# A fused two-layer convolution block on one core: another order of the work inside a chunk, and of GpSimd's step in the second layer

## The chip, the cores and the metric

The kernel runs on one core of a Trainium2 chip. The metric is the device time in microseconds of one execution. Other engines are named as the profile names them: PE (TensorE), DVE (VectorE), ACT (ScalarE), POOL (GpSimd), SP (SyncE, here a DMA queue).

## The reference, cut to what matters

```python
# x: (16, 512, 64, 64) float32
# layer 0
g  = group_norm(x, groups=32)
gs = stack([sum_c(g * shifted(g, di, dj)) for di in range(5) for dj in range(5)])  # 25 maps
gs = gs / sqrt(sum(gs * gs) + 1e-6)
x  = x + relu(einsum(concat([g, gs]), W) + bias)
# layer 1
g  = group_norm(x, groups=32)
s  = relu(w2 @ relu(w1 @ mean_hw(g) + b1) + b2)          # one score a plane
q  = clip(floor(s), 0, 5)
pools = [maxpool_same(g, k) for k in (1, 3, 5, 7, 9, 11, 13)]
x  = x + (s - q) * pools[q + 1] + (q + 1 - s) * pools[q] + g
```

## The kernel before

**Layer 0** takes 16 images, each in 8 chunks (`c`) of 8 rows, so 128 chunks. Each engine runs its own list of instructions in the order in which its `image` function writes them; semaphores tie the lists together. In a chunk, PE does the picks of descriptor rows (L1253), four grams of the next chunk (`gram`, L1208, two PSUM banks in turn, so that gram 2 waits for DVE's first mask and gram 3 for its second), the norm (L1275), the descriptor part of the previous chunk's output (`tail`, L1286), 48 convolution matmuls (L1231 to L1233) and four transposes after the first 12 of them (`turn_blocks`, L1266). DVE multiplies each gram with a mask (L808), finishes the descriptor (L848, L852), takes the statistics of the finished rows (`y_stats`, L820), writes maxima over three columns (`wide_rows`, L829 to L842) and takes the statistics of a later image's x (`x_stats`, L758, four instructions a chunk). In chunk 4 it closes the next image's group statistics (`group_sums`, L768; `group_spreads`, L775 to L781), for which PE waits at L1298. ACT normalises a chunk three ahead (L595, L597), squares and takes roots (L625, L627), applies relu to the output (`conv_out`, L611) and copies the transposes (L618). POOL computes the low halves of the normalised values (`low_parts`, L447), splits the descriptor (L466, L468) and adds the residual in place (L456). Normalised chunks stand in a ring of four, so chunk c+3 may be written only when the convolution of chunk c-1 is done.

**Between the layers** the 8192 planes are sorted by class (0 to 5, the pool size) into 67 tiles of 128 planes; 5 more steps are empty.

**Layer 1** has a step for each tile t. ACT copies its planes into a padded buffer (`pad_plane`, L673 to L675), then writes the results of tile t-2 (`results`, L695, eight instructions), then the diagonals of the tile (L687). DVE pools (`pools`, L1062), PE mixes. POOL's step issues the DMAs: `gather_source(t+1)` fetches the planes of row maxima into the one buffer `source` (index copy L528, indirect DMA L531), `gather(t+2)` fetches the records and planes of y into one of four buffers (L506, index copy L507, then a branch on the class, L511, L514), `scatter(t-1)` writes a finished tile out (L539). `pad_plane(t)` waits for both fetches of its tile and for DVE to have left the padded buffer:

```python
            def pad_plane(t, u):
                act.wait_ge(gathered[u], turns_done(t, u))
                if not (isinstance(t, int) and t == 0):
                    act.wait_ge(s_rows, t)
                act.wait_ge(sourced, (t + 1) * 16)
```

`gather_source(t)` waits until the pad of tile t-1 has read `source` (s_ypad), `scatter(t)` until the eight results of its tile are written (s_res), `gather(t+2)` until the DMA of `scatter(t-2)` has landed.

## Time and profile before

| | us |
|---|---|
| median of 3 runs | 4451.67 (4446.97 to 4456.05) |
| the profiled execution, its own time | 4448.36 |
| its span | 4446.7 |
| PE busy | 3932.6 (88%) |
| DVE busy | 3557.4 (80%) |
| POOL busy | 2279.6 (51%) |
| ACT busy | 1897.6 (43%) |
| granted PE clock, mean of the span | 0.947 of full speed |
| first and last start of the picks (L1253) | 63.2, 2585.9 |
| first and last start of the pads (L673) | 2687.3, 4337.8 |

The span is read in two parts: layer 0 up to about 2610 us, layer 1 from about 2690 us. Shares of busy time are means over both.

### The profile page before, as it was taken

The numbers are of one execution on the slowest core, as the hardware profiler recorded it, in microseconds if no ns is written. First come the engines' busy times: TensorE is split into PE (matmuls) and PEld (weight loads), VectorE is DVE, ScalarE is ACT, GpSimd is POOL, SyncE is SP. The second block draws the span as 40 slices with busy tenths as digits, with TensorE's granted clock in tenths as the row PEclk, the third lists the DMA queues.
The fourth block names the chain that finished last, engine by engine and source line by source line (L and its number), as shares of the span: only waits on it lengthen the run. The fifth ranks groups of instructions, "written<-read, shape, count | busy, mean of one in ns | idle before, by whom it ended". The sixth has DMA issues, their size and how long they took to land. (4 is left out here: it accounts for less than half of the span.)

```text
span 4446.7 us, 76741 instructions
## 1 busy us (share of the span) xinstructions
PE 3932.6 (88%) x23656; PEld 2159.5 (49%) x23657; DVE 3557.4 (80%) x3528; ACT 1897.6 (43%) x2964; POOL 2279.6 (51%) x1793
## 2 busy tenths in 40 slices
PE   5999999999999999999999965789888888888785
PEld 3556555555555555655566642334333333333332
DVE  5878888788887878888888766699866799999993
ACT  3444444444454544444444403443433333433332
POOL 3555555555555655555565514355544444556442
PEclk9999999999999999999999977899998999989897
DMA  4444344544544444444453334545555566565551
GB/s 183 151 173 176 137 168 167 176 150 156 195 149 159 173 150 167 177 150 155 176 173 132 121 79 172 202 174 190 198 219 234 197 234 246 227 243 211 224 212 50
DMA packets 252235, 781.08 MB, mean 176 GB/s; under 512 B 98150, under 2 KB 98150, under 8 KB 229990
## 3 DMA queue, kind: packets, MB, share of 16 engines
q1 hardware_dynamic: 219600, 417.85, 26.9%
q0 software_dynamic: 32288, 358.95, 20.9%
q8 instruction: 176, 2.88, 0.3%
q14 instruction: 171, 1.40, 0.1%
HBM read 428.22 MB, written 409.08 MB: 188 GB/s over the span
## 5 line engine op out<-in xcount | busy, mean ns | idle before, releaser
L1062 DVE TENSOR_TENSOR arena<-arena 128x2048 f32<-128x2048 f32 (+5 forms) x539 | 1442.4, 2695 | 262.2 <-ACT arena L675 223.0
L1403 PE MATMUL psum<-arena 128*128 128x512 f32 x1072 | 608.3, 651 | 293.4 <-ACT arena L695 213.0
L1208 PE MATMUL psum<-arena 128*128 128x256 f16 (+1 forms) x6344 | 754.6, 273 | 57.4 <-DVE arena L808 44.2
L447 POOL TENSOR_TENSOR arena<-arena 128x512 f16<-128x512 f32 x512 | 720.8, 1415 | 147.1 <-ACT arena L597 141.0
L1231 PE MATMUL psum<-arena 128*128 128x512 f16 x2048 | 776.5, 379 | 0.0
L1233 PE MATMUL psum<-arena 128*128 128x512 f16 x2048 | 776.2, 379 | 0.0
L1232 PE MATMUL psum<-arena 128*128 128x512 f16 x2048 | 776.2, 379 | 0.0
L673 ACT ACTIVATE arena<-arena 128x4096 f32 x67 | 242.4, 3619 | 1051.7 <-issue 1051.7
L1208 PEld LDWEIGHTS psum<-arena 128*128 128x128 f16 x6344 | 600.3, 101 | 177.6 <-DVE arena L808 71.7
L456 POOL TENSOR_TENSOR arena<-arena 128x512 f32 (+1 forms) x512 | 635.0, 1272 | 9.0 <-ACT arena L611 6.2
L820 DVE BATCH_NORM_STATS2 bny<-arena 128x6 f32 (+1 forms) x512 | 355.6, 694 | 340.0 <-POOL arena L456 326.7
L611 ACT ACTIVATE arena<-psum,bias_sb 128x512 f32<-128x512 f32 x512 | 338.1, 686 | 581.3 <-POOL arena L456 380.1
L1407 PE MATMUL psum<-arena 128*128 128x512 f32 x1072 | 578.9, 623 | 0.0
L466 POOL CAST arena<-arena 128x128 f16<-128x128 f32 x128 | 37.3, 291 | 999.3 <-DVE arena L852 999.3
L1403 PEld LDWEIGHTS psum<-arena 128*128 128x128 f32 x1072 | 216.1, 208 | 589.7 <-issue 316.7
L1405 PE MATMUL psum<-arena 128*128 128x512 f32 x896 | 494.2, 635 | 0.0
L595 ACT ACTIVATE arena<-arena,gbias,grstd 128x512 f32 (+1 forms) x512 | 413.3, 807 | 48.6 <-POOL arena L447 45.9
L597 ACT ACTIVATE arena<-arena,gbias,grstd 128x512 f16 (+1 forms) x512 | 411.3, 803 | 0.0
L539 POOL DMA_INDIRECT out<-arena x67 | 115.4, 1722 | 544.2 <-issue 544.2
L1407 PEld LDWEIGHTS psum<-arena 128*128 128x128 f32 x1072 | 218.0, 203 | 287.7 <-issue 287.7
L808 DVE TENSOR_TENSOR arena<-psum,cst 128x256 f32<-128x256 f32 x496 | 287.1, 579 | 74.8 <-PE psum L1208 60.3
L695 ACT ACTIVATE arena<-psum,arena 128x512 f32<-128x512 f32 x536 | 319.0, 696 | 57.5 <-PE psum L1407 46.0
(161 smaller groups left out, 4324.0 us busy)
## 6 DMA issues: line engine op xcount, KB each, us to landing
arena<-in_x SPq DMA_DIRECT2D x64, 2048.0 KB, 13.2
wide_planes<-arena SPq DMA_DIRECT2D x128, 1024.0 KB, 5.4
y_planes<-arena SPq DMA_DIRECT2D x64, 2048.0 KB, 7.6
arena<-arena SPq DMA_DIRECT2D x1536, 8.0 KB, 1.8
arena<-wide_planes,arena POOLq DMA_INDIRECT x72
arena<-plane_records,arena POOLq DMA_INDIRECT x67
arena<-y_planes,arena POOLq DMA_INDIRECT x67
out<-arena POOLq DMA_INDIRECT x67, 7.9
```

Of the source, the lines that this page charges most:

```text
L447: pool.tensor_tensor(gl[:, ct, slot], g32[:, ct % 2, :], gh[:, ct, slot], ALU.subtract).then_inc(s_gl, 1)
L456: pool.tensor_tensor(y, y, relu[:, o % 2, :], ALU.add).then_inc(s_added, 1)
L595: act.activation(g32[:, ct % 2, :], piece, ACT.Identity, bias=gbias[:, ct:ct + 1], scale=grstd[:, ct:ct + 1])
L597: act.activation(gh[:, ct, (c % RING) * CW:(c % RING + 1) * CW], piece, ACT.Identity, bias=gbias[:, ct:ct + 1], scale=grstd[:, ct:ct + 1]) ...
L1062: ins = dve.tensor_tensor(dst, a, b, ALU.max)
L1208: return pe.matmul(dst, w, m, start=(k == 0), stop=(k == nk - 1))
L1231: pe.matmul(dst, h, gh[:, ct, slot], start=(ct == 0), stop=False)
L1232: pe.matmul(dst, h, gl[:, ct, slot], start=False, stop=False)
L1233: last = pe.matmul(dst, l, gh[:, ct, slot], start=False, stop=(ct == CT - 1))
L1403: pe.matmul(dst, diag[:, s, 0, :], bufs[:, u, b * CW:(b + 1) * CW], start=True, stop=False)
L1405: pe.matmul(dst, diag[:, s, 1, :], small[:, s, b * ROWS:(b + 1) * ROWS, 1:W + 1], start=False, stop=False)
L1407: pe.matmul(dst, diag[:, s, 2, :], big[:, s, b * CW:(b + 1) * CW], start=False, stop=True)\
```

## The change

Layer 0. ACT normalises the first two quarters of chunk c+3 at the start of chunk c, the third between square and root, the fourth at the end; where c+3 is the next image's first chunk, it stays late. POOL does three low parts, two residual additions, the split of the descriptor, two residual additions and the last low part. PE does the norm after the tail instead of before gram 1. DVE does the descriptor after the second mask instead of the first, the x statistics at the start of a chunk (in chunk 3 one more before the row maxima, in place of two at its end), and `group_sums` in chunk 4 behind two masks. Two copies in `wide_rows` (L831, L840) become a maximum of the same operand with itself. Layer 1. POOL's step fetches row maxima for tile t+2 instead of t+1, first; then it scatters tile t-1; then it waits for the write of tile t-2 and fetches y for tile t+2. `normalise` takes a list of quarters (`cts`) for this.

```diff
@@ -438,42 +438,49 @@
...
+            def halves(i, c):
+                n = i * CH + c
+                half = c % 2
+                pool.wait_ge(s_fn, n + 1)
+                if not (isinstance(i, int) and i == 0 and c < 2):
+                    pool.wait_ge(grouped[half], (i * (CH // 2) + c // 2) * GROUPED)
+                pool.sem_inc(s_issue, 1)
+                pool.tensor_copy(fh[:, half, :], fn).then_inc(s_th, 1)
+                pool.wait_ge(s_th, n + 1)
+                pool.tensor_tensor(fl[:, half, :], fn, fh[:, half, :], ALU.subtract).then_inc(s_t, 1)
             def image(i, first, last):
                 for c in range(CH):
-                    n = i * CH + c
-                    half = c % 2
-                    pool.wait_ge(s_fn, n + 1)
-                    if not (isinstance(i, int) and i == 0 and c < 2):
-                        pool.wait_ge(grouped[half], (i * (CH // 2) + c // 2) * GROUPED)
-                    pool.sem_inc(s_issue, 1)
-                    pool.tensor_copy(fh[:, half, :], fn).then_inc(s_th, 1)
-                    pool.wait_ge(s_th, n + 1)
-                    pool.tensor_tensor(fl[:, half, :], fn, fh[:, half, :], ALU.subtract).then_inc(s_t, 1)
-                    if c > 0:
-                        residual(i, c - 1)
-                    elif not first:
-                        residual(i - 1, CH - 1)
-                    if c + 3 < CH:
-                        low_parts(i, c + 3)
-                    elif not last:
-                        low_parts(i + 1, c + 3 - CH)
+                    ahead = (i, c + 3) if c + 3 < CH else None if last else (i + 1, c + 3 - CH)
+                    soon = ahead and c + 3 != CH
+                    back = (i, c - 1) if c else None if first else (i - 1, CH - 1)
+                    if soon:
+                        low_parts(*ahead, cts=(0, 1, 2))
+                    if back:
+                        residual(*back, outs=(0, 1))
+                    halves(i, c)
+                    if back:
+                        residual(*back, outs=(2, 3))
+                    if ahead:
+                        low_parts(*ahead, cts=(3,) if soon else range(CT))
             for c in range(3):
                 low_parts(0, c)
@@ -545,19 +552,20 @@
             def step(t, u):
-                if not (isinstance(t, int) and t + 1 >= NT):
-                    gather_source(t + 1, (u + 1) % BUFS)
+                if not (isinstance(t, int) and t + 2 >= NT):
+                    gather_source(t + 2, (u + 2) % BUFS)
+                if not (isinstance(t, int) and t < 1):
+                    scatter(t - 1, (u - 1) % BUFS)
                 if not (isinstance(t, int) and t < 2):
                     pool.wait_ge(written[(u + 2) % BUFS], ((t - 2) // BUFS + 1) * 16 if isinstance(t, int)
                                  else turn_of(t, u - 2))
                 if not (isinstance(t, int) and t + 2 >= NT):
                     gather(t + 2, (u + 2) % BUFS)
-                if not (isinstance(t, int) and t < 1):
-                    scatter(t - 1, (u - 1) % BUFS)
             gather(0, 0)
             gather_source(0, 0)
             gather(1, 1)
+            gather_source(1, 1)
             for u in range(BUFS):
                 step(u, u)
             with pool.Fori(1, NT // BUFS - 1) as g:
@@ -621,25 +628,28 @@
+                    ahead = (i, c + 3) if c + 3 < CH else None if last else (i + 1, c + 3 - CH)
+                    soon = ahead and c + 3 != CH
+                    if soon:
+                        normalise(*ahead, cts=(0, 1), first=first)
                     act.wait_ge(s_pick, n + 1)
                     act.activation(sq, psum[:, BANK_A, 0:QW], ACT.Square).then_inc(s_sq, 1)
+                    if soon:
+                        normalise(*ahead, cts=(2,))
                     act.wait_ge(s_norm, n + 1)
                     act.activation(sq, psum[:, BANK_N, 0:QW], ACT.Sqrt, bias=epsd[:, :]).then_inc(s_root, 1)
                     if not first:
                         for o in range(CT):
                             conv_out(n - 1, o)
+                    if ahead and not soon:
+                        normalise(*ahead, cts=(0, 1))
                     if c + 1 < CH:
-                        turn = lambda: after(i, c + 1)
+                        after(i, c + 1)
                     elif not last:
-                        turn = lambda: after(i + 1, 0)
-                    else:
-                        turn = lambda: None
-                    if c + 3 < CH:
-                        normalise(i, c + 3, first=first, between=turn)
-                    elif not last:
-                        normalise(i + 1, c + 3 - CH, between=turn)
-                    else:
-                        turn()
+                        after(i + 1, 0)
+                    if ahead:
+                        normalise(*ahead, cts=(3,) if soon else (2, 3))
                     if c == STATS_AT and not last:
                         group_root(i + 1)
@@ -828,7 +838,8 @@
-                dve.tensor_copy(pairs_m[:, :, :, 0:half + 1:half], y[:, :, :, 0:W:W - 1]).then_inc(s_pairs, 1)
+                dve.tensor_tensor(pairs_m[:, :, :, 0:half + 1:half], y[:, :, :, 0:W:W - 1], y[:, :, :, 0:W:W - 1],
+                                  ALU.max).then_inc(s_pairs, 1)
...
@@ -869,7 +881,15 @@
-                    between = [[lambda: descriptor(i, c)], res[0:1], res[1:2], res[2:4]]
+                    sums = [lambda: group_sums(i + 1)] if c == STATS_AT and not last else []
+                    between = [[], sums + [lambda: descriptor(i, c)], res[0:1], res[1:4]]
+                    if c == 0 and first:
+                        x_stats(1, 0)
+                        x_stats(1, 1)
+                    if c < 5 and left >= 1:
+                        x_stats(i + 1, c + 2 if c < 4 else CH - 1)
+                    elif c > 5 and left >= 2:
+                        x_stats(i + 2, c - 6)
                     if c + 1 < CH:
                         masks_of(i, c + 1, between)
                     elif not last:
@@ -880,21 +900,12 @@
                                 f()
                     if c == 0 and not first:
                         keep_stats(i - 1)
+                    if c == 3 and left >= 1:
+                        x_stats(i + 1, CH - 2)
                     if c > 0:
                         wide_rows(i, c - 1)
                     elif not first:
                         wide_rows(i - 1, CH - 1)
-                    if c == 0 and first:
-                        for e in range(3):
-                            x_stats(1, e)
-                    if c < 4 and left >= 1:
-                        x_stats(i + 1, c + 3)
-                        if c == 3:
-                            x_stats(i + 1, CH - 1)
-                    elif c > 4 and left >= 2:
-                        x_stats(i + 2, c - 5)
-                    if c == STATS_AT - 1 and not last:
-                        group_sums(i + 1)
                     if c == STATS_AT and not last:
                         group_spreads(i + 1)
                         group_values(i + 1)
@@ -1307,13 +1318,12 @@
                         pe.wait_ge(s_gl, (i * CH + min(c + 3, CH)) * CT if c + 1 < CH else ((i + 1) * CH + 2) * CT)
                         gram(nxt[0], PAIRS * nxt[1])
-                    norm(i, c, last)
-                    if nxt:
                         gram(nxt[0], PAIRS * nxt[1] + 1)
                     if c:
                         tail(i, c - 1)
                     elif not (isinstance(i, int) and i == 0):
                         tail(i - 1, CH - 1)
+                    norm(i, c, last)
                     if nxt:
                         gram(nxt[0], PAIRS * nxt[1] + 2)
                         gram(nxt[0], PAIRS * nxt[1] + 3)
```

What moves on the two engines whose order the prediction rests on. POOL in a step of layer 1's loop, before (s_ypad: a pad is done; sourced: row maxima have landed; s_res: results are written; written: a tile's write has landed):

```order
L526 ISA [waits s_ypad]
L528 ISA [waits sourced]
L528 COPY arena<-arena 128x1
L529 ISA
L531 DMA arena<-wide_planes,arena 128x4096 [waits s_src]
...
L506 MEMSET arena 128x4 [waits written3]
...
L511 DMA arena<-plane_records,arena 128x4
L514 DMA arena<-y_planes,arena 128x4096
...
L502 ISA [waits s_res]
...
L539 DMA out<-arena 8192x4096
```

and of the change:

```order
L533 ISA [waits s_ypad]
L535 ISA [waits sourced]
L535 COPY arena<-arena 128x1
L536 ISA
L538 DMA arena<-wide_planes,arena 128x4096 [waits s_src]
...
L509 ISA [waits s_res]
...
L546 DMA out<-arena 8192x4096
...
L513 MEMSET arena 128x4 [waits written3]
...
L518 DMA arena<-plane_records,arena 128x4
L521 DMA arena<-y_planes,arena 128x4096
```

The fetch of y (memory set, records, y_planes), which stood ahead of the write-out, now stands behind it. DVE in chunk 2 of the first image, from the x statistics on, before:

```order
L758 BN_STATS bnx<-arena 128x6 [waits x_loaded2]
L758 BN_STATS bnx<-arena 128x6 x3
L808 TENSOR_TENSOR arena<-psum,cst 128x2x16x8 [waits s_gram,s_pick]
L848 RECIPROCAL arena<-arena 128x128 [waits s_root]
L852 TENSOR_TENSOR arena<-psum,arena 128x128 [waits s_t,s_rinv]
L808 TENSOR_TENSOR arena<-psum,cst 128x2x16x8 [waits s_gram]
L820 BN_STATS bny<-arena 128x6 [waits s_added]
```

and of the change:

```order
L768 BN_STATS bnx<-arena 128x6 [waits x_loaded2]
L768 BN_STATS bnx<-arena 128x6 x3
L818 TENSOR_TENSOR arena<-psum,cst 128x2x16x8 [waits s_gram,s_pick]
L818 TENSOR_TENSOR arena<-psum,cst 128x2x16x8 [waits s_gram]
L860 RECIPROCAL arena<-arena 128x128 [waits s_root]
L864 TENSOR_TENSOR arena<-psum,arena 128x128 [waits s_t,s_rinv]
```

The second mask has moved ahead of the descriptor, and the x statistics stand where they stood, right ahead of the first mask.

## Rows read from the trace of the kernel before

**Rows 1.** The timeline of PE: start, us, line; chunks 0, 4, 5, 6 and the next 0
```profile
1498.18 0.82 PE L1253 MATMUL psum<-arena,cst 128*32 128x48 f32 x48
...
1576.81 0.88 PE L1253 MATMUL psum<-arena,cst 128*32 128x64 f32 x48
1602.01 0.88 PE L1253 MATMUL psum<-arena,cst 128*32 128x64 f32 x48
1620.91 0.88 PE L1253 MATMUL psum<-arena,cst 128*32 128x64 f32 x48
...
1658.01 0.82 PE L1253 MATMUL psum<-arena,cst 128*32 128x48 f32 x48
```

**Rows 2.** The timeline of PE in chunk 4 of the image before
```profile
1424.94 4.46 PE L1208 MATMUL psum<-arena 128*128 128x256 f16 x24 [2.42 <-DVE arena L808]
...
1441.88 0.38 PE L1298 MATMUL psum<-gd,cst 128*128 128x4 f32 x2 [1.55 <-DVE gd L781]
```

**Rows 3.** Table by stretch, classes 0 to 4: length, then PE, PEld, DVE, ACT, POOL
```profile
2735.00:2904.50 169.50, 131.48 (x261) 55.32 (x259) 111.20 (x50) 79.46 (x120) 64.00 (x58) 0.86 0.51 198
2904.50:3133.50 229.00, 202.32 (x436) 87.11 (x435) 213.45 (x78) 99.54 (x150) 130.81 (x70) 0.93 0.48 176
3163.50:3523.00 359.50, 300.29 (x633) 128.52 (x631) 239.95 (x80) 129.12 (x195) 174.91 (x92) 0.91 0.55 216
3523.00:3806.50 283.50, 243.07 (x529) 104.35 (x528) 258.59 (x99) 109.25 (x165) 123.24 (x77) 0.95 0.62 238
3806.50:4094.50 288.00, 248.07 (x520) 106.08 (x520) 273.12 (x88) 109.26 (x165) 172.56 (x77) 0.91 0.58 225
```

**Rows 4.** The timeline of one tile of class 3: start, us, engine, line
```profile
3579.13 4.72 ACT L695 ACTIVATE arena<-psum,arena 128x512 f32<-128x512 f32 x8
3579.46 23.99 DVE L1062 TENSOR_TENSOR arena<-arena 128x4096 f32<-128x4096 f32 x9 [1.99 <-ACT arena L675]
...
3585.51 1.74 POOL L539 DMA_INDIRECT out<-arena  x1 [7.16 <-issue]
3587.26 0.40 POOL L528 COPY arena<-arena 128x1 int32 x1
3588.56 1.24 POOL L531 DMA_INDIRECT arena<-wide_planes,arena  x1 [0.91 <-POOL arena L528]
...
3594.43 0.18 POOL L507 COPY arena<-arena 128x1 int32 x1
3596.21 3.69 POOL L511 DMA_INDIRECT arena<-plane_records,arena  x1 [1.60 <-issue]
3600.21 4.11 POOL L514 DMA_INDIRECT arena<-y_planes,arena  x1 [0.30 <-issue]
3600.72 3.62 ACT L673 ACTIVATE arena<-arena 128x4096 f32 x1 [15.76 <-issue]
...
3605.20 4.42 DVE L1062 TENSOR_TENSOR arena<-arena 128x4096 f32<-128x4096 f32 x1 [1.75 <-ACT arena L675]
```

**Rows 5.** The timeline of one tile of class 2
```profile
3482.82 4.56 POOL L531 DMA_INDIRECT arena<-wide_planes,arena  x1 [0.91 <-POOL arena L528]
...
3493.88 0.99 POOL L514 DMA_INDIRECT arena<-y_planes,arena  x1 [0.30 <-issue]
3495.76 3.62 ACT L673 ACTIVATE arena<-arena 128x4096 f32 x1 [17.61 <-issue]
```

**Rows 6.** Groups by form of DVE in the tile of class 3: xcount, busy us, mean ns
```profile
L1062 DVE TENSOR_TENSOR arena<-arena 128x4096 f32<-128x4096 f32 x3 | 13.3, 4425 | 2.1 <-ACT arena L675 2.0
L1062 DVE TENSOR_TENSOR arena<-arena 128x2048 f32<-128x2048 f32 x2 | 4.5, 2290 | 0.0
L1062 DVE TENSOR_TENSOR arena<-arena 128x1024 f32<-128x1024 f32 x3 | 3.6, 1223 | 0.1
```

**Rows 7.** The timeline of DVE: the x statistics of one chunk
```profile
1399.38 2.47 DVE L758 BATCH_NORM_STATS2 bnx<-arena 128x6 f32 x4
```

**Rows 8.** One line of DVE: its durations (ns, least, median, most)
```profile
L831 DVE COPY arena<-arena x128: 218/1168/1195, 94.1 to 2607.0; 128x64 f32 x104, 128x64 f32<-128x64 f32 x24
```

More of the change, by code:

```diff
@@ L440, in _, with low_parts @@
         def _(pool):
-            def low_parts(i, c):
+            def low_parts(i, c, cts=range(CT)):
                 n0 = (i * CH + c) * CT
                 slot = slice((c % RING) * CW, (c % RING + 1) * CW)
-                for ct in range(CT):
+                for ct in cts:
                     pool.wait_ge(s_gh, n0 + ct + 1)
@@ L448, in low_parts, with residual @@
                                        ALU.subtract).then_inc(s_gl, 1)
-            def residual(i, c):
+            def residual(i, c, outs=range(CT)):
                 n0 = (i * CH + c) * CT
-                for o in range(CT):
+                for o in outs:
                     y = xs(o, c * CW, CW, i % 2)
@@ L581, in group_root, with normalise @@
                 act.activation(grs[:, :], psum[:, BANK_N, CT:2 * CT], ACT.Sqrt, bias=epsg[:, :]).then_inc(s_gsq, 1)
-            def normalise(i, c, first=False, between=None):
+            def normalise(i, c, cts=range(CT), first=False):
                 n0 = (i * CH + c) * CT
-                act.wait_ge(s_newton, 3 * i + 3)
-                if not first:
-                    act.wait_ge(s_chunk_used, i * CH + c - RING + 1)
-                for ct in range(CT):
+                if 0 in cts:
+                    act.wait_ge(s_newton, 3 * i + 3)
+                    if not first:
+                        act.wait_ge(s_chunk_used, i * CH + c - RING + 1)
+                for ct in cts:
                     if not (isinstance(n0, int) and n0 + ct < 2):
@@ L598, in normalise @@
                                    bias=gbias[:, ct:ct + 1], scale=grstd[:, ct:ct + 1]).then_inc(s_gh, 1)
-                    if between and ct == 1:
-                        between()
             def conv_out(chunk, o):
```

3 lines of the change are left out of this document (2 added, 1 removed).

## The prediction

> **What bounds the kernel now.** The page's shares of busy time mix two layers, so I read the table by stretch first, then the timelines. In layer 0 PE bounds: its chunk starts [rows 1] show 18.9 us for a chunk that waits for nothing (1602.01 to 1620.91), and 25.2 us for chunk 4 (1576.81 to 1602.01). The reader should see how little is to be had: seven chunks of 18.9 and one shorter one (of the two from 1620.91 to 1658.01, 37.1 in all, the first takes 18.2) make a floor of 150.5 us, the image takes 159.8, so 9.3 are waits: 6.3 in chunk 4, and 3.0 in chunks 0 to 3 (78.6 less four times 18.9). In chunk 4 PE waits 2.42 for the first mask of DVE, then spends 4.46 on two grams, held up by the second mask, then waits 1.55 for the group spread [rows 2]. Some 0.4 of the 6.3 are small matmuls that stand only there, so the second mask has 6.3 - 2.42 - 1.55 - 0.4, about 1.9.
>
> In layer 1 the engines are less full: per tile 21.2, 22.9, 27.7, 25.8 and 26.2 us in classes 0 to 4 (169.5 over 8 tiles, 229 over 10, 359.5 over 13, 283.5 over 11, 288 over 11), with DVE busy 111, 213, 240, 259 and 273 of these [rows 3]. A loop through four parties sets the period where DVE is idle. It can be followed in one tile of class 3 [rows 4]: DVE starts at 3579.46; ACT writes results until 3583.85; POOL issues the write-out at 3585.51, 1.66 later (its branch on the class), then the index copy, then the fetch of row maxima, done at 3589.80; the next pad starts at 3600.72 and DVE 4.48 after it. Sum: 25.7, the period. The fetch of y in those rows (3596.21 to 3604.32) is for a tile after the one padded at 3600.72, and has a whole period to land.
>
> The same rows show what a POOL instruction costs beside DVE. The write-out ends 0.9 after a DVE instruction's end (4.43 and 2.4 after the start, that is 3586.3, and 3587.25), the index copy ends with the next one (3587.6 against 3587.66), and the fetches that begin inside the last two DVE instructions take 3.69 and 4.11, again to 0.9 past the ends of these, while one that begins when DVE is idle takes 0.99 [rows 4 to 6]. I use this throughout: a copy ends with the DVE instruction in which it begins, an indirect DMA 0.9 us after.
>
> **The change, layer 1.** The fetch of row maxima for tile t+2 now goes ahead of the write-out; it needs the pad of t+1, so it is issued as DVE starts a tile, and no longer waits for results and write-out. That takes it out of the loop. But the fetch of y for t+2 moves from before the write-out of t-1 to behind it. That write-out needs results which ACT writes only after the pad of t+1. So y, which had a period of slack, is now issued in the very period at whose end its tile is padded. The loop becomes: pad, results, write-out, fetch of y (memory set, copy, 1.6 for the branch on the class, records, 0.3, planes), landing, pad. It is longer than the old one by the records' DMA and 0.7 of branch at least. The wait for the write of t-2, which ended the idle time ahead of the old fetch, falls away at no cost.
>
> Worked for class 3, from DVE's start at 0; its instructions end at 4.4, 6.9, 8.1, 9.3, 10.6, 12.9, 15.1, 19.5, 24.0 (one of 4096, one of 2.4 us, three of 1024, two of 2048, two of 4096, in the order of the code, [rows 6]). Index copy: begins with DVE, ends 4.4. Row maxima: from 5.4 to 7.8. Write-out: ready at 6.05, behind that fetch, to 9.05. Copy to 9.3, branch, records from 11.0 to 13.8, planes from 14.1 to 16.0. From the end of the last fetch to the pad: 8.4 in class 2, where the write-out was issued 7 us before it, 10.9 in class 3, where it was just before [rows 4, 5]; the queue is shared, and here three fetches and writes stand within 8 us, so I take 9.9. With 4.5 to DVE's next start: 30.4, against 25.8. By the same steps, classes 0 and 1 (six first instructions of 2.29; write-out to 7.7, copy to 9.2, records to 12.5, planes to 14.7, landing 8.6): 27.8. Class 2 (2.3 four times, then two of 4.43): records fall into the first long one and end at 14.7, planes into the second, 19.1; with 8.6 and 4.5, 32.2. Class 4: planes end at 17.2, with 9.1 and 4.5, 30.8. Class 5 has shorter instructions in the middle: 27.4, below the 28 us that its twelve DVE instructions need (an estimate from the durations by length [rows 6] and the lengths in the code), so no change there.
>
> Sum: 6.6 x 8 = 53, 4.9 x 10 = 49, 4.5 x 13 = 59, 4.6 x 11 = 51, 4.6 x 11 = 51; first tiles, which lose too (about 19 by the same steps), less 9 that class 5's lead over DVE absorbs: 10. In all **+273 us**. PE (243 us busy over 11 tiles of class 3, 22 a tile) stays hidden, and ACT (109, 10 a tile) too [rows 3].
>
> A rule speaks against the slow fetches. In the rows, the two fetches of y under long DVE instructions take 3.69 and 4.11, and alone 0.99 [rows 4, 5]. The Trainium skill, page "SBUF — State Buffer", section "Who interferes with whom", holds that a tensor_tensor contends with GpSimd's reads but does not hold up descriptor generation (it marks the reason as inferred). By that rule the fetches would take 1 us each. The sum for layer 1 would then be the faster rival's below, -18, and not +273. This trace disagrees with it for indirect DMAs, so I go by the rows.
>
> **The change, layer 0.** No work is added or taken away; PE's floor stays. In chunk 4, two x statistics (2.5 each [rows 7]) and the group sums stood ahead of the first mask; one statistic moves ahead of the previous chunk's row maxima (same queue, so it still delays, but chunk 3 has idle time on DVE), the sums go behind two masks. The descriptor goes behind the second mask, so the wait of 1.9 for this mask goes. `low_parts` now run beside x statistics and masks instead of row maxima. What this is worth shows in the first copy of the row maxima: 1168 ns beside POOL, 218 without [rows 8]; its form as a maximum has a price between these two, and with POOL idle it is near the lower one. I expect row maxima to be about 1.7 us shorter a chunk. The norm now stands behind a gram and the tail, about 3 us later, which makes root, relu and residual later and y statistics, by my estimate, about 1 us; 0.7 a chunk is left to DVE. Chunk 4: 1.2 for the first mask, 0 for the second, 1.2 for the spread, 0.4 that always stood there: 2.8 instead of 6.3. Chunks 0 to 3: 0.8 instead of 3.0. Gain 5.7 an image, 14 such images: **-80 us**. Bounds: nothing, and all of it, 9.3 x 14.5 = 135. I take 80, since the masks' lateness is mostly queue ahead of them. Moving the norm, root and relu back costs nothing as long as relu is ready when PE has done its four grams; an estimated 2 us of cover is left there, and some 3 for the descriptor's DMAs ahead of the next tail. If these went, each of 128 chunks would pay the excess.
>
> Sum: +273 - 80 = +193. The profiled execution has 4448.4, 3.3 below the median of the runs, so 4641 profiled and **4644 us** as a median.
>
> **The rivals.**
> 1. Row maxima early wins, y costs nothing (faster): POOL's later fetches are not drawn out. Then the loop is 6.05 + 1.0 + 0.3 + 1.6 + 1.0 + 0.3 + 1.0 + 8.6 + 4.5 = 24.4 in every class, or DVE's own 25 in class 4. Against the old periods: +26, +15, -43, -15, -11, and 10: -18; with -80, 4350 + 3 = 4354. For it: the 0.99 [rows 5]. Against: DVE is in the middle of its tile when y is fetched, as in [rows 4]. It decides for faster below a mean of 1.5 us lost a tile (80 over 53).
> 2. One more DVE instruction is lost by each write-out, so that the fetch of y slips by about 2.5 us a tile: +130 more, 4775. It would be so if POOL's branch began only when the fetch of row maxima is done. In the rows the branch runs while POOL is still busy or idle, so I doubt it.
> 3. Layer 0 gains nothing, since the x statistic still precedes the masks and y statistics come later; layer 1 as forecast: 4724.
> 4. The change does not do what it says in layer 1: y lands in time because ACT's pad is bound by DVE anyway. Class 1 (213 of 229 busy) is nearest to that. Then only layer 0's gain is left, but some loss in classes 0 and 2: about 4450, no change.
>
> **How the numbers follow.** Forecast 0.70, rival 2 0.10, rival 3 0.11, rival 1 0.06, rival 4 0.03. Within the forecast, 1.5 us of error in a tile's loop is 80 us, and layer 0 may gain 50 more or less. The range 4540 to 4730 takes in the forecast's own bounds and rival 3. A measurement here can tell 0.2%, 9 us. Faster 0.06, same 0.02, slower 0.92.
>
> **What would show it.** Right: in the timeline of layer 1, POOL's fetch of y follows the write-out, and the pad starts 8 to 10 us after it ends; DVE's idle time ahead of its pooling, put down to the pad, about doubles; periods of 28, 28, 32, 30, 31 and 28. The row maxima have landed long before. In layer 0, chunk 4 takes some 21.7 us and the image about 154; the first copy's line takes well under 1 us. Wrong: pads that start without a landing just before, class periods unchanged, or fetches of y of 1 us in the middle of DVE's tile. If the sign is right and the size is not, look first at the time from the last fetch to the pad.

## The result, and the profile after

The changed kernel takes **4749.73 us** (median of 4 runs, 4744.19 to 4756.57) against 4452.97 for the kernel before on the same chip: ratio 1.0669, 95% interval 1.065 to 1.0687. The profiled spans are 4742.5 and 4446.7 us. So the sign was right, but the size is +297 us against the forecast's +193, and 4749.73 lies above the range of 4540 to 4730.

The table by stretch, classes 0 to 5 (length, then PE, PEld, DVE, ACT and POOL busy, PE clock, DMA share, GB/s):

```profile
2683.50:2912.50 229.00, 129.85 (x256) 54.79 (x256) 108.77 (x48) 79.46 (x120) 89.64 (x56) 0.78 0.37 147
2912.50:3211.50 299.00, 221.00 (x459) 94.75 (x460) 222.35 (x80) 99.31 (x150) 127.36 (x70) 0.85 0.34 135
3243.70:3663.00 419.30, 299.71 (x624) 128.32 (x624) 233.93 (x78) 127.28 (x195) 197.63 (x91) 0.85 0.50 185
3663.00:4015.50 352.50, 253.04 (x528) 108.29 (x528) 261.55 (x99) 109.24 (x165) 138.28 (x77) 0.86 0.50 191
4015.50:4376.30 360.80, 255.51 (x528) 109.29 (x528) 274.76 (x88) 109.24 (x165) 162.63 (x77) 0.84 0.48 180
4376.30:4646.20 269.90, 207.59 (x432) 89.09 (x432) 245.05 (x108) 89.41 (x136) 101.38 (x63) 0.87 0.52 196
```

The first five answer to [rows 3]: the same tiles (8, 10, 13, 11, 11, and 9 of class 5) and nearly the same busy time of DVE, in stretches longer by 60, 70, 60, 69 and 73 us. No engine has more work; all of them idle more. From the starts of the pads and the ends of POOL's fetches in the timeline, in us per tile (period: from one pad to the next):

| class | period before | forecast | after | end of y's fetch to pad, forecast | after |
|---|---|---|---|---|---|
| 0 | 21.2 | 27.8 | 28.6 | 8.6 | 8.8 |
| 1 | 22.9 | 27.8 | 29.9 | 8.6 | 8.8, in one tile 6.2 |
| 2 | 27.7 | 32.2 | 32.4 | 8.6 | 8.7 |
| 3 | 25.8 | 30.4 | 32.0 | 9.9 | 11.6 |
| 4 | 26.2 | 30.8 | 32.8 | 9.1 | 10.3 to 11.1 in seven tiles, 8.9 to 9.1 in three, 4.2 in one |
| 5 | 27.0 | no change | 30.0 | - | 10.1 |

The wait that grew, from the waits of the whole span (total, times, longest):

```profile
ACT arena L683 <- issue: 1442.5, 67, 63.8
...
DVE arena L1073 <- ACT arena L685: 612.4, 66, 16.8
```

Before, the pad (then L673) idled 1051.7 us ahead of its 67 executions, and DVE 223.0 us for the pad, 42 times. Now DVE waits for the pad in 66 of 67 tiles, and nearly three times as long, where the forecast had it double. "issue" at the pad is a DMA: the one line of the fetch of y names the pad as its waiter, 65 times, with the time from issue to landing below it:

```profile
  ACT arena L683: 1370.8, 65
...
DMA to landing us min/median/max: 6.4/11.0/12.4
```

The loop itself, in one tile of class 3, to be read beside [rows 4]:

```profile
3726.76 3.62 ACT L683 ACTIVATE arena<-arena 128x4096 f32 x1 [21.75 <-issue]
...
3731.23 23.98 DVE L1073 TENSOR_TENSOR arena<-arena 128x4096 f32<-128x4096 f32 x9 [7.73 <-ACT arena L685]
3731.43 4.27 POOL L535 COPY arena<-arena 128x1 int32 x1 [15.98 <-ACT arena L685]
...
3736.60 2.41 POOL L538 DMA_INDIRECT arena<-wide_planes,arena  x1 [0.90 <-POOL arena L535]
3739.32 1.01 POOL L546 DMA_INDIRECT out<-arena  x1 [0.30 <-issue]
3740.33 0.11 POOL L513 MEMSET arena<- 128x4 f32 x1
3740.38 0.30 POOL L514 COPY arena<-arena 128x1 int32 x1
3742.31 2.72 POOL L518 DMA_INDIRECT arena<-plane_records,arena  x1 [1.64 <-issue]
3745.34 1.82 POOL L521 DMA_INDIRECT arena<-y_planes,arena  x1 [0.31 <-issue]
3758.72 3.62 ACT L683 ACTIVATE arena<-arena 128x4096 f32 x1 [22.00 <-issue]
```

DVE starts at 3731.23. POOL issues the row maxima (L538), the write-out (L546), the records (L518) and y (L521), which ends at 3747.16, 15.9 after DVE's start, where the forecast had 16.0. DVE is done at 3755.2. The pad starts only at 3758.72, 11.6 after the fetch of y, and DVE 4.5 after the pad. The row maxima were issued 19.7 us ahead of the pad; they wait for nobody any more.

A tile of class 0, where the forecast's time for POOL was off:

```profile
2745.46 6.82 DVE L1073 TENSOR_TENSOR arena<-arena 128x2048 f32<-128x2048 f32 x3 [15.67 <-ACT arena L685]
...
2751.52 1.65 POOL L546 DMA_INDIRECT out<-arena  x1 [0.54 <-issue]
2752.44 6.82 DVE L1073 TENSOR_TENSOR arena<-arena 128x2048 f32<-128x2048 f32 x3 [0.16 <-DVE arena L1073]
2753.16 0.12 POOL L513 MEMSET arena<- 128x4 f32 x1
2753.21 1.57 POOL L514 COPY arena<-arena 128x1 int32 x1
2757.01 3.19 POOL L518 DMA_INDIRECT arena<-plane_records,arena  x1 [2.23 <-issue]
2760.50 0.98 POOL L521 DMA_INDIRECT arena<-y_planes,arena  x1 [0.31 <-issue]
2770.39 3.62 ACT L683 ACTIVATE arena<-arena 128x4096 f32 x1 [19.43 <-issue]
```

From the copy to the records' fetch, the branch on the class, POOL takes 2.23, not 1.6. The fetch begins at 2757.01, just behind the boundary between two of DVE's instructions (2752.44 and two thirds of 6.82 are 2756.99), and so lasts to 0.9 after the next one's end. The records end 14.7 us after DVE's start, where the forecast had 12.5. So it is in four of the eight tiles of class 0 (periods of 29.0 to 29.5); in the other four the branch takes 2.1 to 2.2 as well, but the fetch begins just ahead of the boundary, y ends at 14.7 as forecast, and the periods are 27.8 to 28.2.

Layer 0. PE's chunk starts in one image (chunks 0, 1, 3, 5 and the next 0):

```profile
1454.42 0.82 PE L1264 MATMUL psum<-arena,cst 128*32 128x48 f32 x48
1475.72 0.88 PE L1264 MATMUL psum<-arena,cst 128*32 128x64 f32 x48
...
1513.55 0.88 PE L1264 MATMUL psum<-arena,cst 128*32 128x64 f32 x48
1553.60 0.88 PE L1264 MATMUL psum<-arena,cst 128*32 128x64 f32 x48
...
1609.84 0.82 PE L1264 MATMUL psum<-arena,cst 128*32 128x48 f32 x48
```

Chunks 1 and 2 take 37.8 together, so 18.9 each. Chunks 3 and 4 take 40.05: chunk 4 needs 21.15 where it needed 25.2 [rows 1]. Chunk 0 needs 21.3 in this image and between 18.2 and 24.7 in the others, 20.5 in the mean, against 20.2 before. The image takes 155.4, against 159.8. From the first chunk's start to the last one's, layer 0 has 2452.8 us (62.5 to 2515.3), against 2522.1: 69 less.

Why chunk 0 gained nothing shows at an image start with a long chunk 0 (24.7 us):

```profile
1762.99 1.23 DVE L846 TENSOR_TENSOR arena<-arena 128x1024 f32<-128x1024 f32 x1 [2.13 <-DMA wide_planes<-arena]
...
1764.04 0.82 PE L1264 MATMUL psum<-arena,cst 128*32 128x48 f32 x48
...
1769.27 2.47 DVE L768 BATCH_NORM_STATS2 bnx<-arena 128x6 f32 x4 [2.08 <-issue]
1771.65 1.01 DVE L818 TENSOR_TENSOR arena<-psum,cst 128x256 f32<-128x256 f32 x2
1772.29 5.30 PE L1219 MATMUL psum<-arena 128*128 128x256 f16 x24 [2.74 <-DVE arena L818]
```

DVE waited 2.13 for a write of row maxima to land, then 2.08 with no releaser at the start of an image, and then did the x statistic of 2.47 ahead of the first mask (L818), for which PE waited 2.74. And the durations of the first copy of the row maxima, to be read beside [rows 8]:

```profile
L841 DVE TENSOR_TENSOR arena<-arena x128: 265/278/1239, 94.8 to 2539.2; 128x64 f32 x104, 128x64 f32<-128x64 f32 x24
```

### The profile page after: what moved, and what is told of

Its sections match the earlier page's. It is cut to its first block and busy times, and to the rows that moved or that the text cites. A ratio compares the mean times of both kernels' runs of the same rounds, so it can differ in the third digit from the quotient of the medians.

```text
span 4742.5 us, 76845 instructions
## 1 busy us (share of the span) xinstructions
PE 3932.9 (83%) x23656; PEld 2185.4 (46%) x23657; DVE 3364.5 (71%) x3528; ACT 1892.0 (40%) x2964; POOL 2257.0 (48%) x1793
## 5 line engine op out<-in xcount | busy, mean ns | idle before, releaser
L1413 PE MATMUL psum<-arena 128*128 128x512 f32 x1072 | 624.6, 667 | 631.3 <-ACT arena L705 590.4
L447 POOL TENSOR_TENSOR arena<-arena 128x512 f16<-128x512 f32 x512 | 651.1, 1277 | 858.0 <-ACT arena L606 856.2
L1219 PE MATMUL psum<-arena 128*128 128x256 f16 (+1 forms) x6344 | 712.3, 270 | 34.8 <-DVE arena L818 21.5
L535 POOL COPY arena<-arena 128x1 int32 (+1 forms) x72 | 192.0, 2667 | 953.7 <-ACT arena L685 939.5
L1219 PEld LDWEIGHTS psum<-arena 128*128 128x128 f16 x6344 | 588.8, 98 | 119.1 <-DVE arena L818 29.2
L1417 PE MATMUL psum<-arena 128*128 128x512 f32 x1072 | 582.0, 626 | 0.0
L1415 PE MATMUL psum<-arena 128*128 128x512 f32 x896 | 503.3, 646 | 0.0
L768 DVE BATCH_NORM_STATS2 bnx<-arena 128x6 f32 (+1 forms) x512 | 314.8, 678 | 35.7 <-issue 25.0
L818 DVE TENSOR_TENSOR arena<-psum,cst 128x256 f32<-128x256 f32 x496 | 275.7, 586 | 79.6 <-PE psum L1219 79.3
## 6 DMA issues: line engine op xcount, KB each, us to landing
arena<-wide_planes,arena POOLq DMA_INDIRECT x72, 10.6
out<-arena POOLq DMA_INDIRECT x67, 12.8
```

The costliest lines, as they stand in the source:

```text
L447: pool.tensor_tensor(gl[:, ct, slot], g32[:, ct % 2, :], gh[:, ct, slot], ALU.subtract).then_inc(s_gl, 1)
L1219: return pe.matmul(dst, w, m, start=(k == 0), stop=(k == nk - 1))
L1413: pe.matmul(dst, diag[:, s, 0, :], bufs[:, u, b * CW:(b + 1) * CW], start=True, stop=False)
L1415: pe.matmul(dst, diag[:, s, 1, :], small[:, s, b * ROWS:(b + 1) * ROWS, 1:W + 1], start=False, stop=False)
L1417: pe.matmul(dst, diag[:, s, 2, :], big[:, s, b * CW:(b + 1) * CW], start=False, stop=True)\
```

## The experiments

Twelve kernels in four groups (e1 to e4, e5 to e8, e9 to e11, e12); each group shared its runs of the kernel before. A ratio below is to those, with its 95% interval.

**e1 and e2, the two halves of the change.** e1 keeps the change's layer 0 and has the old step in layer 1; e2 the other way round.

```diff
 # e1, against the change
-                    gather_source(t + 2, (u + 2) % BUFS)
-                    scatter(t - 1, (u - 1) % BUFS)
+                    gather_source(t + 1, (u + 1) % BUFS)
                     pool.wait_ge(written[(u + 2) % BUFS], ...)
                     gather(t + 2, (u + 2) % BUFS)
+                    scatter(t - 1, (u - 1) % BUFS)
```

> The change's chunk order in layer 0, with the old GpSimd step in layer 1. The two parts lie one after the other, so their effects should add. Theory (the two spans of the trace): first to last picks 2452.8 instead of 2522.1, so 69 us faster than before, 4384 us; class periods in layer 1 as before. Rival (layer 1's loss comes in part from what layer 0 leaves behind): well off 4384.

> Layer 0 as before, with the change's GpSimd step. Theory: before plus the whole loss of layer 1, 365 us: 4818 us; periods of 28.7, 29.9, 32.4, 32.0, 32.8 and 30.0 us in classes 0 to 5. Rival as in e1: off by more than 20 us.

Measured: e1 4385.31 us, 0.9855 [0.9839, 0.9872]; e2 4825.51 us, 1.0848 [1.083, 1.0866]. The halves are -64 and +376 against their before (4449.68), together +312; the whole change has +297. So all of the loss is the step of layer 1, as expected, and the halves add up to within 15 us, a third of a per cent. Some 9 of these are in class 4: in e2 the fetch of y slips into another long instruction of DVE in six tiles (periods of 34.7 to 35.3), in the change in three.

**e3, y a whole tile earlier.** The row maxima still go first, but y is fetched for tile t+3, into the buffer of the tile that has just been written out; the wait is then for that write.

```diff
-                    pool.wait_ge(written[(u + 2) % BUFS], ((t - 2) // BUFS + 1) * 16 ...)
-                    gather(t + 2, (u + 2) % BUFS)
+                    pool.wait_ge(written[(u + 3) % BUFS], ((t - 1) // BUFS + 1) * 16 ...)
+                    gather(t + 3, (u + 3) % BUFS)
```

> The change, but the fetch of y is for tile t+3 and waits for the write of t-1: it stands behind the write-out and still has a whole period. Theory (y in the loop is the whole loss, early row maxima are a gain): periods near DVE's own work or the step's own length, about 21, 23, 22, 24.5, 25.5, 28 us; about 4300 us, below both kernels. Rival (early row maxima are worth nothing, since three transfers then land together): periods as before, 4384 us.

Measured: 4380.44 us, 0.9853 [0.9836, 0.9871]. This undoes 369 us of loss by fetching y one tile further ahead, with the row maxima still first: the theory's mechanism holds. Its number (4300) does not, and the rival's 4384 is met only in the sum, since the periods are not as before. They are 19.8, 22.3, 25.4, 27.4, 28.2 and 27.8: better than before in classes 0 to 2, worse in 3 to 5. One tile of class 3 shows why:

```profile
3604.65 0.10 POOL L513 MEMSET arena<- 128x4 f32 x1 [13.59 <-DMA out<-arena]
...
3606.58 4.85 POOL L518 DMA_INDIRECT arena<-plane_records,arena  x1 [1.61 <-issue]
...
3611.74 2.08 POOL L521 DMA_INDIRECT arena<-y_planes,arena  x1 [0.31 <-issue]
...
3615.14 1.22 POOL L538 DMA_INDIRECT arena<-wide_planes,arena  x1 [0.89 <-POOL arena L535]
```

POOL stands 13.59 us at the landing of the write, then needs 9.2 for y, of which 4.85 go into a fetch under a DVE instruction of 4.42, and only then fetches the row maxima, 13 us ahead of their pad. Here, what stands in front of the last fetch on POOL is in the loop.

**e4, y ahead of the write-out.** Row maxima, then y for t+2, then the write-out.

```diff
                     gather_source(t + 2, (u + 2) % BUFS)
-                    scatter(t - 1, (u - 1) % BUFS)
                     pool.wait_ge(written[(u + 2) % BUFS], ...)
                     gather(t + 2, (u + 2) % BUFS)
+                    scatter(t - 1, (u - 1) % BUFS)
```

> The change, with the fetch of y for t+2 ahead of the write-out of t-1, behind the fetch of row maxima. Theory (both the wait for the pad and the write-out ahead of it lengthen the loop): results and write-out leave the loop, y ends at about 12.5, 12.5, 14.7, 13.8, 15.0 us into DVE's tile, periods 25.6, 25.6, 27.8, 28.2, 28.6, 28 us: about 4520 us. Rival (only the write-out's place counts): periods as before, 4384. Rival (only the place behind the pad counts): no change, 4750.

Measured: 4590.5 us, 1.0318 [1.0301, 1.0335]. Periods 27.7, 27.3, 29.4, 29.0, 29.8 and 27.7. 159 us come back of the loss, less than expected, and neither rival's number is met. One tile of class 0:

```profile
2749.42 6.83 DVE L1073 TENSOR_TENSOR arena<-arena 128x2048 f32<-128x2048 f32 x3 [14.09 <-ACT arena L685]
...
2759.92 1.97 POOL L521 DMA_INDIRECT arena<-y_planes,arena  x1 [0.31 <-issue]
2762.19 1.93 POOL L546 DMA_INDIRECT out<-arena  x1 [0.30 <-issue]
```

The fetch of y ends 12.5 us after DVE's start, and in nearly all tiles of classes 1 to 4 at 12.5, 14.6, 13.8 and 15.0, within 0.1 of the expectation. The miss is the landing: the pad starts 10.0 to 10.8 us after that end in the mean of every class (8.7 to 8.8 in classes 0 to 2 of the change), with the write-out issued 0.3 us behind the fetch. So a transfer behind y also makes it late, and a y fetched after the pad of t+1 stayed in the loop in both places that were tried.

**e5, the long instructions of DVE cut in two**, in the changed kernel.

```diff
+                    if tuple(dst.shape)[1:] == (H, W):
+                        dve.tensor_tensor(dst[:, 0:H // 2], a[:, 0:H // 2], b[:, 0:H // 2], ALU.max)
+                        dst, a, b = (v_[:, H // 2:H] for v_ in (dst, a, b))
                     ins = dve.tensor_tensor(dst, a, b, ALU.max)
```

> The change, with each pooling instruction of 4096 elements cut into two of 2048. Theory (a GpSimd copy ends with the DVE instruction in which it begins, an indirect DMA 0.9 us after): y is fetched earlier by about 2 us in some tiles of class 1, 4.4 in class 2, 2 in classes 3 and 4: 110 us faster than the change, about 4640. Rival (pooling does not hold up the making of descriptors): the length of DVE's instructions does not matter, 4750 or a few us more for the added instructions.

Measured: 4653.58 us, 1.0457 [1.044, 1.0473], 96 us less than the change (110 expected), with the same work for DVE and none less for POOL. One tile of class 3:

```profile
3720.87 2.14 POOL L535 COPY arena<-arena 128x1 int32 x1 [16.27 <-ACT arena L685]
...
3723.90 2.16 POOL L538 DMA_INDIRECT arena<-wide_planes,arena  x1 [0.89 <-POOL arena L535]
...
3730.55 1.66 POOL L518 DMA_INDIRECT arena<-plane_records,arena  x1 [1.62 <-issue]
3732.52 1.96 POOL L521 DMA_INDIRECT arena<-y_planes,arena  x1 [0.31 <-issue]
```

The copy that lasted 4.27 beside an instruction of 4.43 lasts 2.14 beside one of 2.29, and the fetch of y ends 13.8 us after DVE's start instead of 15.9. So DVE's tensor_tensor does hold up POOL's index copies and its indirect DMAs. The Trainium skill, page "SBUF — State Buffer", section "Who interferes with whom", which keeps descriptor generation out of that, is not borne out for indirect DMAs here. Class 2 gained 2.3 us a tile and not 4.4: y is fetched earlier, as expected, but now 6.9 us behind the start of the write-out instead of 9.0, and its landing rises from 8.7 to 10.6.

**e6, the write-out taken away**, in the changed kernel.

```diff
-                    pool.indirect_dma_start(out=out_rows[:, :],
-                                            out_offset=bass.IndirectOffsetOnAxis(ap=idx[:, b:b + 1], axis=0),
-                                            in_=bufs[:, b, :], in_offset=None,
-                                            bounds_check=NPL - 1, oob_is_err=False).then_inc(written[b], 16)
+                    pool.dma_start(no_out[bass.ds(t, 1), :], bufs[0:1, b, 0:REC]).then_inc(written[b], 16)
```

> The change, but the second layer's result is not written out: the write-out of a tile is a DMA of 16 bytes. Theory (three transfers share the queue, and the write-out just ahead of the fetch of y makes this land late): the time from the end of the fetch of y to the pad falls from 11.6 to about 8.6 us in classes 3 and 4, from 10.7 to about 9 in class 5, none in classes 0 and 1; the whole some 80 to 110 us shorter than the change, 4640 to 4670. Rival (landing is slow by itself): 11.6 stays, 4740.

Measured: 4498.96 us, 1.0116 [1.0097, 1.0136]. One tile of class 3:

```profile
3655.37 0.55 POOL L546 DMA_DIRECT2D no_out<-arena  x1
...
3661.69 1.83 POOL L521 DMA_INDIRECT arena<-y_planes,arena  x1 [0.30 <-issue]
3672.19 3.62 ACT L680 ACTIVATE arena<-arena 128x4096 f32 x1 [19.11 <-issue]
```

From the end of y's fetch to the pad are 8.7 us in this tile, and 8.4 to 8.8 in the mean of every class, class 3 among them (11.6 with the write). In class 3 POOL's fetch of y ends 15.9 us after DVE's start with the write and without it, so the write in front of y costs 2.9 us of landing there. But the whole fell by 251 us, not by 80 to 110, and most of that is not landing. In classes 0, 1 and 2, where the landing was 8.7 to 8.8 already, the periods also fell, by 3.0, 4.6 and 4.6 us. There the write-out held up POOL's own list: without its 1.7 to 1.9 us the records' fetch begins 2.5 to 3 us earlier, and y ends at 12.4 instead of 14.7 or 16.0 (class 0) and at 14.7 instead of 19.1 (class 2), at least one instruction of DVE earlier. The expectation had left this out.

**e7 and e8, layer 0 in parts.** e7 is the kernel before with the two copies of the row maxima as maxima; e8 is e1 with the two copies as they were before.

```diff
-                dve.tensor_copy(pairs_m[:, :, :, 0:half + 1:half], y[:, :, :, 0:W:W - 1]).then_inc(s_pairs, 1)
+                dve.tensor_tensor(pairs_m[:, :, :, 0:half + 1:half], y[:, :, :, 0:W:W - 1], y[:, :, :, 0:W:W - 1],
+                                  ALU.max).then_inc(s_pairs, 1)
```

> The kernel before with only the two copies of the row maxima as a maximum of the operand with itself. Theory (a copy waits for GpSimd, a maximum does not, in the trace of the change 278 ns against 1168): DVE is 0.9 us earlier a chunk, which shortens the waits of chunks 0, 1 and 4 by up to 0.9 each and the spread's: 25 to 50 us faster. Rival (a maximum with both inputs in SBUF waits for GpSimd as well, and the 278 ns come from the new order): within 0.2% of before.

> Layer 0 in the change's order, but with the two copies; layer 1 as before. Theory (the gain comes from the second mask ahead of the descriptor and from GpSimd's low parts moved away from the row maxima): 50 to 69 us faster than before. Rival (the gain is the maxima's): within 20 us of before.

Measured: e7 4450.1 us, 1.0006 [0.9997, 1.0016]; e8 4405.49 us, 0.9904 [0.989, 0.9918]. In the old order the maximum lasts as long as the copy did:

```profile
L831 DVE TENSOR_TENSOR arena<-arena x128: 273/1224/1257, 94.2 to 2607.8; 128x64 f32 x104, 128x64 f32<-128x64 f32 x24
```

In e8 the plain copy has a median of 214 ns. So it is the order that brings the 1168 ns of [rows 8] down, and not the form. In three images of the changed kernel (1454 to 1924 us) POOL is idle in 16 of the 17 short executions, of 0.28 us, and the 7 long ones, of 1.2, all lie beside one of its low parts (L447). Still the form is worth 20 us in the new order (4405 to 4385), all in chunk 0 (22.3 against 21.0 us in the mean). The trace puts 13 of the 20 in DVE's time without a releaser at the start of an image, 3.2 us each in e8 and 2.1 in e1 (38.0 and 25.1 us in all, 12 times). What these are was not tried, nor what each single move of the order is worth.

**e9, the x statistic of chunk 0 later**, in e1.

```diff
-                    if c < 5 and left >= 1:
+                    if 0 < c < 5 and left >= 1:
...
                         wide_rows(i - 1, CH - 1)
+                    if c == 0 and left >= 1:
+                        x_stats(i + 1, 2)
```

> The change's layer 0 with the old POOL step of layer 1 (e1, 4385 us), and one x statistic moved: in chunk 0 it stands behind the row maxima instead of ahead of the masks. Theory (what is left in chunk 0 is DVE's queue ahead of the first mask: at the image's start DVE waits about 2 us for the loop itself and 2 us for a write of row maxima to land, and then the x statistic of 2.5 us still precedes the mask): the 2.5 us go from most of the 14 image starts, chunk 0 takes about 19.3 us instead of 21.0, and the time is 4360 to 4366. Rival (chunk 0 is late for the landing of the row maxima's write, and the statistic behind them only makes the next one late): 4385, unchanged.

Measured: 4407.59 us, 0.9899 [0.9883, 0.9914], 22 slower than e1, so theory and rival both missed. Chunk 0 falls to 18.8 in nearly every image, as the theory had it. But chunk 1 rises from 18.9 to 21.2 or 22.9:

```profile
1785.10 0.82 PE L1265 MATMUL psum<-arena,cst 128*32 128x48 f32 x48
1803.95 0.88 PE L1265 MATMUL psum<-arena,cst 128*32 128x64 f32 x48
1811.62 4.46 PE L1220 MATMUL psum<-arena 128*128 128x256 f16 x24 [2.12 <-DVE arena L817]
```

Chunk 0 here takes 18.85, and in chunk 1 PE waits 2.12 for the first mask and then spends 4.46 on two grams that take 2.79 otherwise. Both theory and rival had only chunk 0 in view. DVE is behind at an image start in both orders, and a statistic moved past the masks makes the next ones late. The x statistic of chunk 1 stands at its head, so that with this edit two stand in a row ahead of chunk 1's first mask.

**e10, e11 and e12, towards a faster version.** e10 is e1 with e5's cut; e11 is e3 with the cut and with e9's late statistic; e12 is e3 with the cut alone.

```diff
 # e12, against e3
+                    if tuple(dst.shape)[1:] == (H, W):
+                        dve.tensor_tensor(dst[:, 0:H // 2], a[:, 0:H // 2], b[:, 0:H // 2], ALU.max)
+                        dst, a, b = (v_[:, H // 2:H] for v_ in (dst, a, b))
```

> The change's layer 0 with the old POOL step (e1, 4385 us), and each pooling instruction of 4096 elements cut in two. Theory (an indirect fetch that begins inside a DVE instruction ends 0.9 us after it, here the fetch of row maxima of class 2, 4.56 us long): class 2 gains some 1.6 us a tile, the others nothing to speak of, DVE pays 0.15 us for each cut: 4360 to 4370. Rival (with the old step the fetch in the loop is short anyway, and DVE bounds classes 3 to 5): 4385 to 4395.

> The change's layer 0 with the late x statistic, the fetch of y for a tile further ahead (e3, 4380 us), and the long pooling instructions cut in two. In e3 POOL waits 13.6 us for the landing of a write and then loses 6.9 us to the two fetches of y, of which 4.9 lie in a long DVE instruction, before it can fetch row maxima. Theory: the cut takes 2 us of that from each tile of classes 3 and 4 and the late statistic 20 us in layer 0: 4320 to 4335. Rival (the landing of the write sets the period of classes 3 to 5, and DVE gets dearer by 0.3 us a tile): 4355 to 4365.

> As e11, but the x statistic of chunk 0 stands where the change put it. Theory (layer 1's gain of e11 and layer 0's of the change add, since layer 0's late statistic cost e9 22 us against e1): 4357 - 22 = 4335. Rival (the sum is not additive, layer 1's start depends on the state in which layer 0 leaves the queues): 4350 to 4360.

Measured: e10 4367.05 us, 0.9809 [0.9791, 0.9827]; e11 4357.2 us, 0.9787 [0.9774, 0.98]; e12 **4335.75 us**, 0.9755 [0.9741, 0.9768]. In e10 class 2 goes from 27.8 to 26.0 a tile (13 tiles, 23 us), and its fetch of row maxima from 4.56 [rows 5] to 2.42. In e11 the cut takes 1.8 and 2.3 us a tile off e3's classes 3 and 4, as the theory had it, while the late statistic costs layer 0 some 22, as in e9, instead of gaining 20; so the time falls where the rival had it, for another reason. Without the late statistic the 22 come back in e12, at the number expected. One of its tiles of class 3:

```profile
3509.45 0.10 POOL L513 MEMSET arena<- 128x4 f32 x1 [13.06 <-DMA out<-arena]
...
3511.07 2.29 DVE L1075 TENSOR_TENSOR arena<-arena 128x2048 f32<-128x2048 f32 x1 [0.86 <-ACT arena L686]
3511.87 2.44 POOL L518 DMA_INDIRECT arena<-plane_records,arena  x1 [1.61 <-issue]
```

The records' fetch takes 2.44 instead of 4.85, and DVE idles 0.86 us ahead of its tile: with periods of 25.8, 26.0 and 26.9 in classes 3 to 5, DVE, busy 24.0, 24.8 and 26.5 of them, is nearly the bound. This version beats both kernels of the case.

## Why the prediction was right or wrong

The mechanism was right: the loop is pad, results, write-out, fetch of y, landing, pad; the row maxima are out of it; PE and ACT stay hidden. e2 puts all the loss there, e3 takes it away by moving y alone. In the spans the whole is +296: layer 0 -68, the first tiles +16, classes 0 to 5 +60, +70, +62, +69, +73 and +27 (periods by tiles), the tail -13. Three terms of layer 1 were mis-sized; they make 95 of the 104 us by which the forecast was short.

- **The landing of y in classes 3 and 4.** The step "the queue is shared, and here three fetches and writes stand within 8 us, so I take 9.9" failed. POOL's part in class 3 was right to 0.1 us (15.9 against 16.0), and so it was in most tiles of class 4; the landing was 11.6 in class 3 (9.9 taken) and 10.3 to 11.1 in seven tiles of class 4 (9.1 taken). I took a value between two old landings (8.4 and 10.9) though neither had three transfers of 2 MB in a row. Which tiles have all three can be read off the GB/s of the first table. 185 GB/s over 419.3 us and 191 over 352.5 are 6.0 and 6.1 MB a tile in classes 2 and 3, but 147 over 229 and 135 over 299 only 4.2 and 4.0 in classes 0 and 1, so there row maxima move no data ([rows 3] have the same: 198 over 169.5 is 4.2 MB a tile in class 0, 238 over 283.5 is 6.1 in class 3). With the write alone ahead of y (class 0) the landing is 8.8, with row maxima alone (e6, class 3) 8.7, with both 11.6. With both, but the write started 9.0 us before y instead of 6.0 (class 2), it is 8.7 again, and with 7.1 us, in seven tiles of class 4, 10.3 to 11.1. In class 3 the term is 1.7 x 11 = 19 us, in these seven tiles of class 4 1.5 x 7 = 11. The rest of class 4's error of 22 is three tiles in which y slipped into another long instruction, to end at 21.6 instead of 17.2: their landing is the forecast's (8.9 to 9.1), and their periods are 34.9 to 35.1.
- **"Class 5 ... so no change there."** 27.4 a tile was held against 28 that DVE needs. With a landing of 10.1 instead of 8.6 and 2.1 to 2.5 instead of 1.6 for POOL's branch the loop has 30.0, above DVE's 28: 27 us that the sum had at nothing. A margin of 0.6 us under a bound was no ground for a zero, when 1.5 us of error was admitted a few lines on.
- **Classes 0 and 1.** "Records to 12.5, planes to 14.7": the branch took 2.1 to 2.6 us, not 1.6, so in half of the tiles the records' fetch began just past a boundary of DVE and lasted one instruction more, to 14.7, and in class 0 the fetch of y to 16.0. In the other half the step came out as forecast. Landing was right (8.8). In class 1 four of the ten periods are 27.9 to 28.0 and five 32.2 to 32.6, as y's own fetch lasts 1.8 us or, in a long instruction, 4.1. This is the kind of slip of rival 2, in a quarter of its size and at another place (the branch's length, not its start): +7 and +21.

Class 2 was right (32.4 against 32.2), for the reason given. The wait for the write of t-2 fell away at no cost, as said. First tiles and tail together came to +3 instead of the +10 of the sum.

**Layer 0** gave 69 of 80. The descriptor behind the second mask and the sums behind both did what they were to do: chunk 4 has 21.1 where 21.7 was forecast, with 1.5 for the spread and nearly nothing for masks. The step "chunks 0 to 3: 0.8 instead of 3.0" failed in chunk 0 alone (chunk 1 fell by 1.0, as its share of that was). At an image start DVE stands 2 us without a releaser. The rows read did not show that; the trace before has 1.3 us of it (14.5 us in all, 11 times), behind the x statistic and right ahead of the first mask. In the change DVE also waits up to 2.1 us there for a write of row maxima to land (20.5 us in all, 17 times), and the 2.5 us of statistic still stand ahead of the mask. The price of the first copy fell to 278 ns as said, and e8, where the plain copy has 214, shows that POOL's order does it and not the form (e7: no gain by the form in the old order). The whole new order is worth 41 us by itself and the form 20 on top.

**The rule** that the prediction weighed against the rows did not hold here. Fetches of y of 1 us under DVE's long instructions were not seen (4.1 in class 2), and with instructions half as long the fetches shortened and 96 us came back (e5). Rival 1 is out by that, rival 3 by e1, rival 4 by the periods.

The errors in layer 1 went one way: a landing from the middle, a branch at the value of the old order, class 5 from a comparison just won. The range had 1.5 us of error a tile, as large as the errors turned out in the mean of classes 0 to 5, but it was laid on the 53 tiles of classes 0 to 4 alone.

## What to carry to other kernels

When a fetch is moved to make room for another, ask in which period it is issued and in which it is needed: the fetch that moves out of the loop frees nothing if the one that takes its place is issued a period later than before. Price a landing by what stands ahead of it and behind it in the same queue in the new order, and not by the mean of the old ones. Where GpSimd issues indirect DMAs beside a DVE that is always busy, shorter DVE instructions shorten the fetches; how much of that reaches the time depends on the order around them (96 us in the changed kernel, 18 in e10, 45 from e3 to e12).

## What the runs showed of the hardware

- The landing of the fetch of y, 2 MB by the queue of the indirect DMAs, from the end of its instruction to the pad that waits: 8.7 to 8.8 us with one other transfer of 2 MB in the 10 us ahead of it, be it a write (class 0) or a fetch (e6); 11.6 with both, the write started 6.0 us before the fetch of y (class 3), and 8.7 with both and 9.0 us between them (class 2); 10.4 to 10.8 in the mean with only a write issued 0.3 us behind it (e4, classes 0 and 1).
- The write-out's own time to landing has a median of 7.9 us where it stands behind the fetch of y and ahead of that of row maxima (before, e1), 12.8 where it stands between row maxima and y (after), 13.0 right behind both (e4), and 14.0 in e3. A buffer that is freed by that landing comes 5 to 6 us later.
- POOL's branch on the class, between the index copy and the records' fetch, took 1.5 to 1.6 us before in all tiles of classes 0 to 5 but one (4.0), whether the copy ahead of it lasted 0.2 or 3.5 us. In the changed kernel it took 1.6 to 1.7 behind a copy of 0.3 (class 3), 1.8 to 2.1 behind one of 1.3 (class 2, one tile 2.5), 1.8 to 2.5 behind one of 1.4 (class 4) and 2.1 to 2.6 behind one of 1.5 to 1.8 (classes 0, 1 and 5). In e3 it is 1.6 again, also behind copies of 4.0. The rows of before do not show that, and the cause stays open.
- The landing of row maxima written in layer 0 went from 5.4 to 8.9 us in the median with the new order, and DVE waited for it 20.5 us in all, in 17 chunks.
- A maximum of an operand with itself in place of a copy changes nothing in its own duration beside a busy POOL (1224 against 1168 ns), and gains 20 us in another place of the program (e8 against e1), for a reason that stays open.
- The mean granted PE clock, between its levels of 2.4 GHz (1.0) and 1.2 GHz (0.5), was lower where PE idled more (0.95 before, 0.86 after in class 3), and PE's busy time a tile rose from 22.1 to 23.0 us; it stays hidden.
